# Narrow heads: PV of a rank's first key block in two halves by query columns, around the next transposed scores

## What is computed

```python
def _L1_attn_ref(x, Wq, Wk, Wv, Wo):
    B, S, D = x.shape
    H, hd = 16, D // 16                     # 16 heads of 8
    q = (x @ Wq.T).reshape(B, S, H, hd).transpose(0, 2, 1, 3)
    k = (x @ Wk.T).reshape(B, S, H, hd).transpose(0, 2, 1, 3)
    v = (x @ Wv.T).reshape(B, S, H, hd).transpose(0, 2, 1, 3)
    ...
    scores = jnp.einsum('bhcd,bhsd->bhcs', qi, k) * scale
    scores = jnp.where(mask, scores, jnp.finfo(scores.dtype).min)
    p = jax.nn.softmax(scores, axis=-1)
    out = jnp.einsum('bhcs,bhsd->bhcd', p, v)
    ...
    return out @ Wo.T
```

## Time and profile before

| | |
|---|---|
| time, median of 3 runs | 4629.71 us (4620.19 to 4632.78) |
| time of the profiled execution | 4618.62 us |
| its span | 4616.8 us |
| mean granted TensorE clock | 0.987 |
| mixed layers and heads, about | us 70 to 1216 |
| pass 1, about | us 1230 to the end |

### The profile page before, as it was taken

One profiled execution on the slowest core, in us unless ns is written; L12 is line 12 of the kernel. 1 busy time (PEld: TensorE's weight loads), 2 busy tenths in 40 slices (PEclk: granted clock), 3 DMA queues, 4 the chain that ended last, 5 costly groups with the idle time before them and its releaser, 6 DMA issues. The chain is left out here.

```text
span 4616.8 us, 170264 instructions
## 1 busy us (share of the span) xinstructions
PE 4360.6 (94%) x67636; PEld 2560.0 (55%) x67636; DVE 3281.1 (71%) x5769; ACT 2763.3 (60%) x5481; POOL 2197.2 (48%) x1996
## 2 busy tenths in 40 slices
PE   7999999998699999999999999999999999999995
PEld 4555555555355555555555555555555555555553
DVE  4656666565477777777777777777777777777773
ACT  4544555445366666666666666666666666666663
POOL 0000000000366666666666766666666666666671
PEclk9999999999899999999999999999999999999997
DMA  1000000000121112211121112111122111221112
GB/s 38 8 6 8 8 6 6 6 8 3 40 58 45 47 47 67 53 42 48 48 67 48 48 48 63 52 48 49 48 59 55 48 48 43 67 53 43 48 48 65
DMA packets 145049, 189.52 MB, mean 41 GB/s; under 512 B 34151, under 2 KB 66298, under 8 KB 144250
## 3 DMA queue, kind: packets, MB, share of 16 engines
q1 hardware_dynamic: 144250, 178.39, 14.3%
HBM read 29.39 MB, written 4.19 MB: 7 GB/s over the span
## 5 line engine op out<-in xcount | busy, mean ns | idle before, releaser
L1351 POOL TENSOR_TENSOR cs<-cs 128x512 f32<-128x512 f32 x768 | 979.6, 1276 | 547.9 <-DVE cs L1661 547.1
L1470 PE MATMUL psum<-wqkv,xw 128*128 128x512 f32 x2304 | 1191.1, 609 | 31.2 <-POOL xw L1388 24.8
L1661 DVE TENSOR_TENSOR cs<-psum,rots 128x1024 f32<-128x1024 f32 x768 | 937.6, 1221 | 245.3 <-PE psum L1470 235.4
L1360 POOL TENSOR_TENSOR qk<-cs,rn 128x512 f32<-128x512 f32 x768 | 776.5, 1042 | 331.1 <-ACT rn L1536 285.5
L1552 ACT ACTIVATE sq<-psum 128x512 f32<-128x512 f32 x768 | 458.8, 597 | 629.7 <-DVE cs L1661 599.1
L1386 POOL MEMSET qTl<- 128x2048 f32 x1 | 1.8, 1804 | 1200.4 <-POOLq L507 1200.4
L1615 DVE TENSOR_REDUCE ss<-sq 128x8 f32<-128x512 f32 x768 | 519.7, 677 | 6.8
L1421 PEld LDWEIGHTS psum<-pT,vw 64*64 64x64 f32 x18624 | 401.0, 135 | 186.3 <-issue 185.8
L1475 PEld LDWEIGHTS psum<-ident,qk 128*128 128x128 f32 x3088 | 352.8, 141 | 262.2 <-issue 151.9
L1475 PE MATMUL psum<-ident,qk 128*128 128x128 f32 x3088 | 443.0, 278 | 48.4 <-DVE state L1695 31.5
L1470 PEld LDWEIGHTS psum<-wqkv,xw 128*128 128x128 f32 x2304 | 368.7, 190 | 194.9 <-issue 170.1
(11 more groups left out here) (205 smaller groups left out, 6809.3 us busy)
## 6 DMA issues: line engine op xcount, KB each, us to landing
vw<-vl SPq DMA_DIRECT2D x768, 128.0 KB, 2.4
vw<-vl SPq DMA_DIRECT2D x672, 64.0 KB, 2.0
wqkv<-in_wqkv SPq DMA_DIRECT2D x42, 256.0 KB, 3.7
wol<-in_wol SPq DMA_DIRECT2D x7, 512.0 KB, 4.3
w1l<-in_w1l SPq DMA_DIRECT2D x7, 341.0 KB
xin<-in_x SPq DMA_DIRECT2D x9, 256.0 KB, 2.9
xr<-in_x SPq DMA_DIRECT2D x8, 256.0 KB, 2.9
sums<-sumout SPq DMA_DIRECT2D x8, 256.0 KB, 2.3
```

The costliest lines, as they stand in the source:

```text
L1351: summed_rot.done(nc.gpsimd.tensor_tensor(own, own, halves(cs[:, t % 2, j, 1, :])[:, :, ::-1, :], ALU.add), at)
L1360: rotated.done(nc.gpsimd.tensor_tensor(qk[:, j, :].rearrange("p (h c) -> p h c", c=EL), cs[:, t % 2, j, 0, :].rearrange("p (h c) -> p h c" ...
L1470: last = nc.tensor.matmul(ps[:, :], xw[:, t * P:(t + 1) * P], wqkv[:, col:col + BANK], start=True, stop=True)
L1661: parts.done(V.tensor_tensor(cs[:, t % 2, j, :, :].rearrange("p i (h c) -> p i h c", c=EL), twice, by_head, ALU.mult), at)
```

## The change

A new step `bq r` stands in each of the four ranks between `bs r+1 2` (in rank 3: `bt 3 0`) and `bt r 1`. It waits for `acc` to be free, in rank 0 for v1, and for all four exponentials of `bt r 0`, and issues PV of key block 0 for the query columns 0 to 255. `bp r 0`, at its old place behind `bt r 1`, issues only the columns 256 to 511 and waits for nothing more. Both halves go to the same bank; only the first has the start flag. ScalarE and VectorE have no part in `bq`, and the ring is as it was.

```diff
@@ -260,7 +260,7 @@
     for r in range(RANKS):
         first, second, third = [[("bs", r + 1, i)] if r + 1 < RANKS else [] for i in reversed(range(1, T))]
         out += [("bn", 0)] + first if r == 0 else first + rest_of(r - 1)
-        out += [("bt", r, 0)] + second + [("bt", r, 1), ("bp", r, 0)] + third + [("bp", r, 1), ("bt", r, 2)]
+        out += [("bt", r, 0)] + second + [("bq", r), ("bt", r, 1), ("bp", r, 0)] + third + [("bp", r, 1), ("bt", r, 2)]
         out += [("bo", r - 1)] if r else []
         out += [("bn", r + 1)] if r + 1 < RANKS else []
     return out
@@ -761,20 +761,30 @@
+                elif kind == "bq":
+                    r = at[0]
+                    free_acc(it, ("oe", r))
+                    settle(pe, passed)
+                    if r == 0:
+                        pe.wait_ge(copied.sem, copied.value(it, ("v1",)))
+                        settle(pe, passed)
+                    pe.wait_ge(exped_b.sem, exped_b.value(it, ((r, 0), RANKS - 1)))
+                    settle(pe, passed)
+                    for g in range(RANKS):
+                        nc.tensor.matmul(acc[32 * g:32 * g + 32, 0:N // 2], v1a[:, 0, 4 * g + r, :], pb[:, 0, g, 0:N // 2],
+                                         start=True, stop=False, skip_group_check=True)
                 elif kind == "bp":
                     r, j = at
-                    if j == 0:
-                        free_acc(it, ("oe", r))
+                    if j:
+                        pe.wait_ge(exped_b.sem, exped_b.value(it, ((r, min(j, 2)), RANKS - 1)))
                         settle(pe, passed)
-                    if at == (0, 0):
-                        pe.wait_ge(copied.sem, copied.value(it, ("v1",)))
-                        settle(pe, passed)
-                    pe.wait_ge(exped_b.sem, exped_b.value(it, ((r, min(j, 2)), RANKS - 1)))
-                    settle(pe, passed)
                     for g in range(RANKS):
-                        last = nc.tensor.matmul(acc[32 * g:32 * g + 32, j * P:N], v1a[:, j, 4 * g + r, :],
-                                                pb[:, j % 2, g, 0:N - j * P] if j < 3 else pb[:, 0, g, 2 * P:3 * P],
-                                                start=(j == 0), stop=(j == T - 1), skip_group_check=True)
+                        if j == 0:
+                            columns, src = slice(N // 2, N), pb[:, 0, g, N // 2:N]
+                        else:
+                            columns, src = slice(j * P, N), pb[:, j % 2, g, 0:N - j * P] if j < 3 else pb[:, 0, g, 2 * P:3 * P]
+                        last = nc.tensor.matmul(acc[32 * g:32 * g + 32, columns], v1a[:, j, 4 * g + r, :], src,
+                                                start=False, stop=(j == T - 1), skip_group_check=True)
```

## The result

The changed kernel takes 4639.93 us, the kernel before 4627.49 us (medians of 17 runs each). The ratio is 1.0030 with a 95% interval of 1.0023 to 1.0038, so it is 10.6 to 17.6 us slower. On a second occasion (experiment e9) it was 1.0032 (1.0019 to 1.0044), 4639.5 against 4624.61. The forecast was 4653 us, the range 4634 to 4669. The direction was right, and the size 13 us too large.

The account below looks back on a forecast made before the run. TensorE was taken as the bound, busy 4360.6 of 4616.8 us. Ranks 0 to 2 (-5.0), the last ranks (+15.6) and the clock (+13) sum to +23.6 us; from the 4629.71 us median that gave 4653 us, range 4634 to 4669.

Parts of the forecast that it names:

- Ranks 0 to 2: Narrow heads: the first half PV fills TensorE's pause before `bt` 1; 24 ranks gain 0.21 us each, -5.0 us.
- The last rank: Rank 3 of each sample: the new wait delays `bt` 1, and `bt` 2 comes 1.95 us later; 8 times, +15.6 us.
- The sum of the order: Narrow heads, without the clock: -5.0 us in ranks 0 to 2 and +15.6 in the last ranks give +10.6 us.
- The clock: Behind the last rank's pauses TensorE's clock falls in 5 to 6 of 8 samples: 5.5 times 2.4 us, +13 us.
- the 2.4 us: Forecast cost of one clock fall in the last rank, half speed less what ScalarE's fixed 1.64 us hides.
- rows 8: Profile rows before the change: one sample's clock fell to 1.2 GHz after pauses of 0.94 and 0.61 us, costing 2.70 us.
- The base: The time before the change to which the forecast was added: the median of three timed runs, 4629.71 us.
- the second rival: Faster: the wide heads hide the last rank's delay, -5 to -9.4 us, up to -15; 4622 us, chance 0.06.
- the first rival: The last rank is delayed but the clock stands: +10.6 us, 4640 us, chance 0.23.
- the prediction's other reading: Skill section on loop structure: a long DMA wait breaks the warmth, PSUM copies don't; no fall added, sum stops at +10.6.

Follow-up runs that it names:

- e9: The changed kernel itself, run again on one chip beside two other runs, against the kernel before: 4639.5 us, 1.0032.
- e1: The changed kernel with `bq` in ranks 0 to 2 only, the last rank in its old order: 4620.14 us, 0.9985 of before.
- e8: `bq` in ranks 0 to 2 only, PV cut at 128 columns in place of 256, last rank as before: 4616.69 us, 0.9987 of before.
- e3: The changed kernel with both PV halves back to back behind `bt` 1 in all ranks: 4627.75 us, 1.0003 of before.
- e6: The kernel before with the whole PV of block 0 ahead of `bt` 1 in ranks 0 to 2: 4629.42 us, 1.0014 of before.
- e2: The changed kernel with `bq` in the last rank only, ranks 0 to 2 as before: 4649.24 us, 1.0047 of before.
- e5: The kernel before with only one wait more: last rank's `bt` 1 waits for all four exponentials of `bt` 0: 4648.57 us, 1.0058 of before.
- e4: The changed kernel with eight filling products in the last rank's pause in front of `bq`: 4636.9 us, 1.0020 of before.
- e10: The changed kernel with eight filling products in the last rank's pause, repeated beside the changed kernel on one chip: 4634.32 us, 1.0020 of before.
- e11: The kernel before with the added wait before the last rank's `bt` 1 and eight filling products in that pause: 4639.4 us, 1.0031 of before.
- e7: `bq` in ranks 0 to 2 only, and in the last rank `bt` 2 ahead of PV of block 1: 4609.99 us, 0.9970 of before.

## Why the prediction was right or wrong

**Ranks 0 to 2: right.** A half was put at 0.57 us and took 0.57. `bt` 1 was to be 0.21 late and is (4.12 against 3.91), the period was to be 12.85 and is 12.85. e1 shows the -5.0 alone (-5.1 by trips, -7.3 by medians), e8 agrees with the account that it is the filled pause less one change of step, e3 shows that the cut has no price of its own. That the first exponential of `bt` 1 sits right behind, so that a bigger first piece would lose, was said in passing; e6 showed it.

**The last rank: right.** The cause, the place and the 1.95 us are as forecast (7.81 in place of 5.86), and nothing of it was recovered: e2's trips are longer by the whole 1.95. e5 shows that the wait alone makes 1.54 of the 1.95; the first half behind it makes the rest, as the forecast's sum had it.

**The sum of the order, +10.6 us: right.** e4 and e10 measured +9.5 and +9.7 us with the clock held in the last ranks.

**The clock: right in kind, priced too high.** The forecast was 5.5 falls of 2.4 us, +13 us. The trace of the changed kernel has seven falls in the eight last ranks and that of e9 six, a few more than forecast. The eleven that can be read cost 0.65 to 2.03 us, 1.23 in the mean. With the seventh sample by its place (8.91 and 8.62 where 7.81 is undisturbed) they come to 8.7 and 6.7 us. The medians give +3.0 and +5.2 us, and their intervals allow the traces' values too. So the 13 us were too large by a factor of 1.5 to 2 by the traces and of 2.5 to 4 by the medians.

The term that failed is the 2.4 us. It was taken from the one fall in rows 8, but that fall was no odd one. In rank 0 of samples 1 to 7 the same fall came once in before, twice in e2 and once each in e3 and e11, and cost 2.70 us each time (period 15.38 or 15.39 in place of 12.68). What failed was to carry this price to another place. Behind the last rank's pause the clock was back in half the time in five of the seven. Four of them can be read and cost 0.65 to 1.38 us; the two that lasted as long as the one in rows 8 cost 1.98 and 2.03. Other falls come and go in both kernels (before had one in rank 0 of the seventh sample, the changed one had one in the third and one in the eighth), which blurs the medians by as much.

**The base** was chosen from three runs at 4629.71; with seventeen it is 4627.49, 2 us of the 13. The other 11 are the clock: by the medians 12.4 - 10.6 leaves 1.8 us for it. One slip in the prediction: the second rival's -9.4 adds up to -9.2, which changes nothing.

So the result stands between the forecast and the first rival: the clock does fall, as against the rival, yet the time came out at the rival's 4640 us, which was itself reckoned from a base 2 us too high. That the result lies inside the range says little of the clock's term, since the range let it be anything from nothing to all. By the profile alone (+21.7 against +23.6) the forecast looks better than it is, since 4 us of that lie in pass 1, where the profile before was faster than the other twelve: that closeness is luck.

In the traces a pause of 2.08 us is followed by the lower clock in seven of eight last ranks (six of eight in e9, two of eight in e2), and where it was filled there is no fall in 24 (e4, e10, e11). The Trainium skill's section "A second HAM failure mode: psum-queue depth-cycling" (page "TensorE: Matmul & The Clock Gate") describes a clock that swings because TensorE stands idle for short times between groups of matmuls. The trace agrees in kind, with the 2.08 us; the pause here is a wait for exponentials. No DMA wait was in play, so the prediction's other reading, that no fall would be added, did not come true. Why the same pause brings the clock down in seven, six or two of eight is open.

## What to carry to other kernels

A step put into a loop over ranks meets a different neighbourhood in the last turn: check there what stands between the new wait and the work it waits for. Here three ranks gained 0.21 us each and the fourth lost 1.95. A pause on an in-order engine is filled by a piece of later work whose inputs are ready inside the pause; cutting costs one change of step (0.14 us here, on e3's evidence), and the piece must be small enough that what the next step feeds on another engine does not come late. Here the step was best left out of the last turn (e1), with the two steps there exchanged as well (e7). Price a fall of the clock for the place where it will come: in rank 0, with the pause unfilled, it cost 2.70 us each time, behind the last rank's pause 0.65 to 2.03.

## What the runs showed of the hardware

- Four products of 32 partitions' columns cut in two cost 1.00 us back to back and 0.57 each apart (0.99 whole): the 0.14 us goes with standing between other kinds of step.
- The same wait in front of `bt` 1 (e5) released TensorE 3.71 us after `bt` 0, and in front of `bq` 3.55. The first has the waits for its banks behind it. That this is the cause of the 0.16 was not tried.
- The clock fell after pauses of about 2 us in seven of eight places in the changed kernel, six of eight in e9, seven of eight in e5 (2.23 us) and two of eight in e2, and in none of 24 where the pause was filled.
- In rank 0 of samples 1 to 7, where `bt` 1's pause is unfilled, five falls cost 2.70 us each (before, e2, e3, e11). Where PV fills it, nine falls cost 1.22 to 1.30 us each (the changed kernel, e1, e6, e8, e9, e10; 13.70 in place of 12.46 in the changed kernel), and the clock was back in half the time. The cause was not tried.
